# Attention: queries and keys as f32 rows, 32 to a head, in place of stacked bf16 parts

## The reference

```
B, S, E = (2, 512, 256)          # the model runs it on 4 sequences of 1024
H, DC, DR = (16, 64, 128)
HD = E // H

def _apply_rope(x, cos, sin):
    d = x.shape[-1]
    x1, x2 = (x[..., :d // 2], x[..., d // 2:])
    rot = jnp.concatenate([-x2, x1], axis=-1)
    return x * cos + rot * sin
```

## Time and profile before

| | us |
|---|---|
| median of three runs | 5604.66 |
| lowest and highest | 5599.1, 5614.04 |
| profiled execution, its time | 5588.05 |
| profiled execution, its span | 5586.3 |
| of it, the attention stage, about | 4041 to 5119 |

### The profile page before, as it was taken

The page is one execution under the profiler, slowest core; times in us unless marked ns, Lnnn a source line. Parts: engine busy times, 40 slices in busy tenths (PEclk is TensorE's granted clock), DMA queues, the critical chain, the costliest instruction groups (busy, mean ns, idle before and its releaser), DMA issues.

```text
span 5586.3 us, 49157 instructions
## 1 busy us (share of the span) xinstructions
PE 4036.1 (72%) x14620; PEld 2267.8 (41%) x14620; DVE 2891.1 (52%) x5797; ACT 2218.7 (40%) x4003; POOL 2525.7 (45%) x2140
## 2 busy tenths in 40 slices
PE   6887887659757787977757599665847777778592
PEld 2333333447525455753323266443612222234362
DVE  6888999711256642118878422361244545454322
ACT  5565655101166651115534133221424444544141
POOL 5888999520134431029877522453041422222504
PEclk9899999679878888988878799867957877787796
DMA  6777655312201102324544311312441222211134
GB/s 177 195 202 197 174 143 149 100 55 96 67 15 26 27 17 72 96 78 129 137 114 127 114 46 46 104 48 75 143 99 35 50 39 39 41 30 52 61 108 134
DMA packets 382865, 510.64 MB, mean 91 GB/s; under 512 B 39946, under 2 KB 237103, under 8 KB 382527
## 3 DMA queue, kind: packets, MB, share of 16 engines
q1 hardware_dynamic: 337076, 410.50, 27.2%
q0 software_dynamic: 33984, 86.32, 5.2%
q10 hardware_dynamic: 11520, 10.49, 0.5%
HBM read 375.42 MB, written 138.28 MB: 92 GB/s over the span
## 4 chain that ended last, share of the span: by engine, by line
PE 34%; DVE 8%; POOL 7%; issue 7%; ACT 5%; DMA 4%; another core or an unknown queue 2%; SPq 1%; DVEq 0%; POOLq 0%; ACTq 0%
PE s_gate_up L2148 7%; PE s_result_sum L2164 3%; PE s_hidden_sum L1570 2%; PE s_result_sum L1581 2%; PE s_out_sum L3463 2%; PE s_scores_T L3450 2%; POOL s_gathered L963 2%; PE s_scores L3414 2%; PE s_shared L2824 2%; POOL s_h L435 2%; DVE s_decay L370 1%; ACT s_weights_T L3269 1%; DMA s_rows<-sorted_rows 1%; PE s_bank L2063 1%
## 5 line engine op out<-in xcount | busy, mean ns | idle before, releaser
L477 PE MATMUL s_y_sum<-s_h,identity 128*128 128x512 f32 x1536 | 798.6, 657 | 254.7 <-POOL s_h L444 224.1
L435 POOL TENSOR_TENSOR s_h<-s_dtu,s_bc 128x1024 f32<-128x1024 f32 x384 | 901.5, 2358 | 107.5 <-PE s_y_sum L477 48.8
L402 ACT ACTIVATE s_decay<-s_dt,s_A 128x512 f32<-128x512 f32 x768 | 498.4, 682 | 392.4 <-DVE s_h L377 385.8
L477 PEld LDWEIGHTS s_y_sum<-s_h,identity 128*128 128x128 f32 x1536 | 301.6, 208 | 707.2 <-POOL s_h L444 340.6
L3269 ACT ACTIVATE s_weights_T<-s_scores_T 128x1024 f32<-128x1024 f32 (+3 forms) x384 | 300.1, 812 | 411.1 <-PE s_scores_T L3450 408.4
L2148 PE MATMUL s_gate_up<-s_w_gate_up,s_rowsT 128*128 x1184 | 424.1, 491 | 16.7 <-issue 16.2
L963 POOL DMA_INDIRECT s_gathered<-sorted_results,pick_row x192 | 199.5, 1039 | 491.9 <-SPq L113 421.9
L3333 POOL TENSOR_SCALAR_AFFINE_SELECT s_weights_T<-s_weights_T 128x256 f32<-128x256 f32 x256 | 104.0, 409 | 633.3 <-ACT s_weights_T L3269 631.1
L2207 DVE TENSOR_TENSOR s_mid<-s_act,s_gate_up 128x128 f32<-128x128 f32 (+1 forms) x228 | 92.8, 407 | 495.9 <-ACT s_act L2180 495.9
L370 DVE TENSOR_TENSOR_SCAN s_decay<-s_decay,s_carry,s_h 128x512 f32<-128x512 f32 x256 | 323.4, 1278 | 47.5 <-POOL s_clip_flag L2520 22.2
L444 POOL TENSOR_TENSOR s_h<-s_h,s_bc 128x512 f32<-128x512 f32 x256 | 325.2, 1271 | 37.9 <-DVE s_h L370 21.3
(11 more groups left out here) (524 smaller groups left out, 7997.8 us busy)
## 6 DMA issues: line engine op xcount, KB each, us to landing
s_bc<-s_bc_rows SPq DMA_DIRECT2D x384, 512.0 KB
sorted_results<-s_result SPq DMA_DIRECT2D x228, 128.0 KB
s_rows<-sorted_rows SPq DMA_DIRECT2D x160, 128.0 KB
rows_by_expert<-zeros SPq DMA_DIRECT2D x16, 1024.0 KB
s_w_inter<-in_L_ffn_experts_inter SPq DMA_DIRECT2D x16, 1024.0 KB
s_w_exp_out<-in_L_ffn_experts_out SPq DMA_DIRECT2D x16, 1024.0 KB
s_queries<-parts_of_q SPq DMA_DIRECT2D x96, 128.0 KB
s_keys<-parts_of_k SPq DMA_DIRECT2D x96, 128.0 KB
```

The lines of the kernel that those rows point to most:

```text
L402: S.e.activation(self.decay[:, (2 * g + d) % 4, :], dt[q // self.passes % 2][:, at, :], ACT.Exp, scale=A[:, at, g % ns:g % ns + 1]).then_i ...
L435: G.e.tensor_tensor(self.h[r][:], dtu[q // self.passes % 2][:, at:at + 2, :], mid(self.bc[r][:, 0, :], 2), ALU.mult).then_inc(*self.fed.up())
L477: made = T.e.matmul(self.y[:, d, :], ident[:], self.h[r][:, d, :], start=False, stop=g % ns == ns - 1)
```

## The change

Queries and keys are no longer split. They stay in f32, in tiles `[128, 2, 1024]` in which each of four heads has 32 rows of its own: 16 of its channels, one for the ones or the maximum, 15 unused. The second index is the group of four heads. The weights of the projections are laid out for this on the host (`in_rows`), with zeros in the unused rows, so the latent expansion and the rotation compute 256 output rows instead of 128. There are three buffers of queries and of keys (`AHEAD`) instead of two.

With it go the splits on ScalarE and GpSimd, both staging DMAs and the loads. The maxima are copied once instead of split, stored in f32, and loaded in four copies, one for each head's row; the ones are loaded for each unit, in four copies. The rotation multiplies with the sine before it takes the other half, so the crossing copies go, and all its steps run on 128 rows twice. In the maxima the order of blocks becomes: two heads by turns, then the other two.

The core of the diff:

```
-    Q_PARTS, K_PARTS = (0, 0, 1, 0, 2, 1), (0, 1, 0, 2, 0, 1)
-    ROWS = 6 * HD
+    ROW = 32
+    AHEAD = 3
...
-    SCORES = [(j, qt, half) for j in range(NG) for qt, half in BLOCKS]
+    SCORES = [(j, qt, half) for pair in range(0, NG, 2) for qt, half in BLOCKS for j in (pair, pair + 1)]
...
-    TURN, LATENT, ACTED, ROPE = ((10, 11), (14, 15)), (18, 20), (22, 24), ((2, 4), (26, 28))
-    ROPED, SPLIT = ((8, 12), (31, 35)), (((30, 32, 34, 36, 38), (31, 33, 35, 37, 39)), ((13, 14, 15, 16, 17), (36, 37, 38, 39, 40)))
+    TURN, LATENT, ACTED = ((10, 11), (14, 15)), (18, 20), ((22, 23), (25, 26))
+    ROPE, ROPED, SMOOTHED = (((2, 3), (4, 5)), ((26, 27), (28, 29))), (8, 32), ((15, 16), (40, 41))
...
+        def ones(u):
+
+            Q.wait_ge(*activated["k"].at(ready(u)))
+            for j in range(NG):
+                Q.e.dma_start(KS[u % AHEAD][j * ROW + HD:j * ROW + HD + 1, :, :], W["const_ones_rows"]).then_inc(
+                    *ones_here[u % AHEAD].dma())
...
-            f = bank[B.of["max", u, a]][0:NG * KT, 0:P]
-            then(V.e.tensor_copy(mP[a][:, 0, :], f))
-            then(V.e.tensor_tensor(mT[:], f, mP[a][:, 0, :], ALU.subtract))
-            then(V.e.tensor_copy(mP[a][:, 1, :], mT[:]))
-            then(V.e.tensor_tensor(mT[:], mT[:], mP[a][:, 1, :], ALU.subtract))
-            V.e.tensor_copy(mP[a][:, 2, :], mT[:]).then_inc(*max_split.up())
+            V.e.tensor_copy(mT[a][:], bank[B.of["max", u, a]][0:NG * KT, 0:P]).then_inc(*max_copied.up())
...
+                    for a in range(2):
+                        yield ACTED[c2][a]
+                        for j, n in enumerate("qk"):
+                            f = take(("act", u, j, c2, a), activated[n].at(6 * b + 2 * c2 + a))
+                            T.e.matmul(f, w_c[HALF[n], a * P:(a + 1) * P], latent[HALF[n], c2 * CH:(c2 + 1) * CH],
+                                       start=True, stop=True).then_inc(*act_sum.up())
...
-                T.e.matmul(f[:, 0:n_keys], QS[u % 2][0:ROWS, h, qt * P:(qt + 1) * P],
-                           KS[u % 2][0:ROWS, h, half * CH:half * CH + n_keys], start=True, stop=True).then_inc(*scored.up())
+                T.e.matmul(f[:, 0:n_keys], QS[u % AHEAD][rows(j, HD), a, qt * P:(qt + 1) * P],
+                           KS[u % AHEAD][rows(j, HD), a, half * CH:half * CH + n_keys],
+                           start=True, stop=True).then_inc(*scored.up())
...
-                h = hg * NG + 2 * pair + i
-                made = T.e.matmul(st[pair][:, i, o:CH], KS[u % 2][:, h, kt * P:(kt + 1) * P],
-                                  QS[u % 2][:, h, qh * CH + o:(qh + 1) * CH], start=True, stop=True)
+                j = 2 * pair + i
+                made = T.e.matmul(st[pair][:, i, o:CH], KS[u % AHEAD][rows(j, HD + 1), hg, kt * P:(kt + 1) * P],
+                                  QS[u % AHEAD][rows(j, HD + 1), hg, qh * CH + o:(qh + 1) * CH], start=True, stop=True)
```

More of the change, by code:

```diff
@@ L3061, in sync @@
             if u + 2 < n_units:
-                stage(u + 2)
-                stack(u + 2, 0)
+                ones(u + 2)
             if 0 <= u + 1 < n_units:
@@ L3253, in project @@
+                for a in range(2):
+                    yield SMOOTHED[j][a]
+                    S.wait_ge(*rope_added.at(4 * b + 2 * j + a))
+                    rotated = of[n][u % AHEAD][:, a, :]
+                    S.e.activation(rotated, rotated, ACT.Gelu).then_inc(*activated[n].up())
         def project(b):
@@ L3334, in main @@
                 beside(2 * s + 1)
-        program(main, combine=sums, front=front, rope=rope, split=split, project=project)
+        program(main, combine=sums, front=front, rope=rope, project=project)
     def tensor():
```

219 lines of the change are left out of this document (95 added, 124 removed).

## The result

The changed kernel takes 6321.67 us (four runs, 6318.77 to 6325.47), the kernel before 5602.24 (four runs beside them and earlier, 5599.1 to 5614.04): a ratio of 1.128, 95% interval 1.1261 to 1.13. The forecast was 5635 with a range of 5520 to 5750. It was wrong, and not by a little: the time lies 570 us above the range, and 370 above rival D, the one that named the cause.

What follows compares the result with a forecast made beforehand. TensorE was taken as the attention stage's fullest engine, but far from full and slow. Columns 636 us at clock 0.87 (731), ends 61, idle 170, chain 15: 977 for 925, +52, start -22: +30, 5635 us; range 5520 to 5750.

Steps and rivals of the forecast that it cites:

- rival D: Attention stage: few rows do not lift the clock, 636 us of columns at 0.6; +344, 5949 us; chance 0.12 with E.
- the clock: TensorE's mean granted clock in the eight attention units: denser work lifts it from 0.79 to 0.87, 636 us becoming 731.
- A: Main forecast, attention units: pairs of heads overlap unrelated pairs, three slots for four, columns 636 us; +30, 5635 us; chance 0.38.
- B: Rival, attention units: pairs only, no overlap with unrelated pairs, columns 756 us at clock 0.92; +86, 5691 us; chance 0.24.
- pipeline ends: TensorE busy time in the attention units beyond columns and clock: 61 us before, kept at 61 in the forecast.
- P: Attention's product with the values (L3463), four heads abreast: 17.8 us a unit at full clock.
- M: Score matmuls only for the row maxima (L3414): 15.8 us a unit before; with S 62.3 as pairs, 46.7 with overlap.
- S: Score matmuls that feed the exponentials (L3450): 15.8 us a unit before; with M 62.3 as pairs, 46.7 with overlap.
- changes of mode: TensorE in attention: some 16 more tiling-mode changes a unit, 22 us more if each lost a full pipeline end.
- The waits: TensorE's idle time in the attention units: 237 us less 20 (maxima's DMA), 12 (splits) and 35 (VectorE), to 170.
- The start: Start of the attention stage: splits, staging and the ones' wait go; -22 us, between -8 and -35.
- Rival E: Attention units: no row groups at work, 1236 us of columns at 0.95; +515, 6120 us; chance 0.12 with D.

Runs made afterwards that it cites:

- small kernel: Computes nothing of the model; repeats one kind of matmul from rest or after bf16 matmuls, 1999.04 us. A second one repeats whole steps, 1366.54 us.
- step mix: Stretches in the second small kernel: whole steps of f32 score matmuls, then the product with the values, nothing to wait for; that kernel took 1366.54 us.

## Why the prediction was wrong

**The step that failed is the clock.** "The clock: denser work should lift it; I take 0.87". It was 0.53. The work did become denser (busy 89% of the units for 74%), and the clock fell: density was the wrong quantity, read from rows in which the scores cover 96 rows or more. The columns are not measured by themselves, so the sum of the units is made with either price of the prediction. Before: 495 of columns, 132 for the clock, 61 of ends, 237 idle. Now, by A: 636 of columns, 636/0.53 - 636 = 564 for the clock, 269 for the rest of the busy time, 185 idle. The difference is +141, +432, +208 and -52, together +729. By B: 756, 670, 43 and 185, so +261, +538, -18 and -52. In either the clock is the largest term. With 0.87 in its place, and the other measured terms as they are, it would have cost 95 (A) or 113 (B), and the whole would have been 5853 or 5765.

**A second term failed with it.** Both of these still lie above the 5750 at which the range ends. So by this sum the range would have missed even with the forecast clock: either the 61 us of pipeline ends were far too few (269 by A), or the overlap of unrelated pairs did not come (B).

**Rival D had the mechanism and the wrong argument against it.** It took 0.6 and 636 of columns, and got 5949. The row against it was that "a busy P has only a quarter of the columns in each matmul" and holds 1.00. Columns of the array are not rows: P of four heads together fills all 128 columns and covers all rows, and from rest it rises by itself. D needed a price for 16-row matmuls at a known clock. The earlier trace rows had the one group of 17 rows in the trace, 674 ns a pass "on the mean of both clocks", and could not give it: 56 of these 64 matmuls ran at the full clock (613 ns each) and 8 at the lower (1096), scattered among other work. If anything they spoke against D. D's price was low besides: it kept 61 of ends and took 0.6.

In the Trainium skill, "TensorE: Matmul & The Clock Gate", Part 1 (The HAM clock gate), the throttle is released by an engine that is busy, and no rows are named. That a busy engine is needed no run here contradicts; but 16-row matmuls that kept TensorE busy without a gap for 41.3 us did not get the full clock, and the measurement decides.

**Row groups side by side: right, and more than right.** In the small kernel four groups take 41.34 us for 41.32 of one. The kernel shows pairs too, and M beside an S of other groups (TensorE in order of time):

```profile
4187.65 1.22 PE L3388 MATMUL s_scores<-s_keys,s_queries 16*128 16x512 f32 x2
4187.66 1.22 PE L3425 MATMUL s_scores_T<-s_queries,s_keys 17*128 17x512 f32 x2
```

The 3.07 times for four row tiles of the Trainium skill, "TensorE: Matmul & The Clock Gate", Part 3 (Packing small matmuls), which would have put the time nearer B, isn't borne out in a stream of equal matmuls: here it is 4.0, with 16 rows at half clock and with 32 rows at full (192 records in 20.88 us, 48 on 64 rows in 20.86).

**A or B: the overlap came, in the main.** The step mix alone has A's three slots, 3.79 us from P to P at full clock where 3.5 (A) and 4.3 (B) had been told apart. In the kernel the busy times of S and M, 519 and 649 us in the units, cover 960 together: they overlap by 207. With S four abreast ahead of M, where only pipeline ends can overlap, it is 42. The 165 between are about three quarters of what A has at this clock (120/0.53 = 226). The run with S four abreast speaks for A as well. Its columns are not in doubt: by the prediction's prices 633 us, 1172 at 0.54, and TensorE is busy 1422, so 250 are neither columns nor clock. A leaves 269 of the changed kernel's 1469 in the same way, B only 43. So the term that was too small beside the clock is the 61 us of pipeline ends, kept from before; this is an estimate from prices, and what makes up the 250 is open. The small kernel's 0.38 us a step would be 73 us in 192 steps. Whether the changes of mode, which the prediction priced at 22 us and left out, are part of it is not shown.

**The waits: right.** TensorE's wait for the maxima's DMA, 27.8 us in the earlier trace rows, is gone from the list, and the five splitting steps with it. The store takes 1.4 us before the loads follow, with nothing ahead, as said from the earlier trace rows:

```profile
4271.49 0.31 SPq L3039 DMA_DIRECT2D max_of_rows<-s_max_rows  x1
4272.90 1.10 SPq L3043 DMA_DIRECT2D s_queries<-max_of_rows  x4
```

There are 62 table loads (31, 12, 12 and 7 at four lines of ScalarE). Idle time was put at 170 and is 185, of 237: apart from the splitting steps the waits for VectorE fell by 15 of some 90 us where 35 had been forecast, and those for ScalarE rose from 97 to 108. ScalarE's total is 11 us more for "net -7: nothing".

**The start: wrong in size.** The first S comes at 4182.9 for 4179.2, and the stage itself begins 5.5 us later for reasons before it (first load of weights at 4041.00, 4035.55 before), so the start gained 1.8 us and not 22. In the stretch 4124 to 4168 one sees why: VectorE, which was to stay its limit with 39 of 44 us busy, is at 26.07, and TensorE at 35.32 for 29.43. The splits and DMAs went, as said, and M in f32 at a clock of 0.64 took their place.

**Rival E**, no groups at work, was priced at 1236 of columns and a clock of 0.95, 6120 in all. The run on all rows one after another is that kernel: 0.96 and 6178. The price was near; that this is quicker than the groups side by side is what no rival had.

## What to carry to other kernels

A matmul on few rows is cheap only if the rest of the stream covers the array: before splitting heads into row groups of 16 rows, run a small kernel with the stream as it will be, from rest and from full clock, and price both levels. A few matmuls of that height among others do not tell: in the trace before they mostly had the full clock. Where rows are free, cover them with zeros (here -242 us for 15 rows of zeros in each group), or stack what belongs together, as the bf16 parts on 96 rows do. And a busy share read from the trace did not forecast the clock for instructions of another height: 74% busy went with 0.79 before, 89% with 0.53 after.

## What the runs showed of the hardware

- From rest, f32 matmuls on one, two, three or four groups of 16 rows stay at 1.2 GHz for all of 41 us, and bf16 on one group too; bf16 on two or four groups does for the 20.7 us that were tried.
- 64 rows in all, as one matmul or two groups of 32, stay as well (41.33 us). 96 in all rise: bf16 on 96 rows, f32 in two groups of 48 or four of 24 (23.04, 23.07, 24.31 us). So do four groups of 32 rows, and 128 rows with data in 16 (22.98, 22.86). No count between 64 and 96 was tried.
- The level depends on where one comes from: started at full clock, four groups of 16 rows keep it (20.88 us), one, two and three groups lose it on the way (35.90, 36.71, 35.82), and the whole 16-row step keeps it.
- Four row groups run entirely abreast in f32: 192 records in 41.34 us, 48 in 41.32.
- More columns at full clock can beat fewer at half: 1236 us of columns at 0.96 took 143 us less than the changed kernel, whose columns are 636 to 756 at 0.53.
